# A perceiver block on one core: other steps for the interleaved stages of a batch, and a program of its own for the last batch's tail

## What is computed

```python
def _layernorm(x, eps=1e-05): ...
def cross(x, ctx):                      # x (4, 256, 256), ctx (4, 4096, 256), 16 heads of 16
    Q = x @ Wq.T + bq; K = ctx @ Wk.T + bk; V = ctx @ Wv.T + bv
    return softmax(Q K^T / sqrt(16)) V @ Wh.T + bh
def linear(x):                          # causal, random features
    q, k, v = split(x @ Wqkv + bqkv)
    def features(t):                    # R = 2, M = 32: 64 features for a head
        tn = t / norm(t)
        return exp(clip(tn @ omega[r] * sqrt(2 s[r]) - s[r], -20, 20)) / sqrt(M) * sqrt(weight[r])
    qf, kf = features(q), features(k)
    # out[t] = sum over t' <= t of (qf[t] . kf[t']) v[t'], over the same sum without v
    return out @ Wout + bout
def ffn(x):                             # integer weights x 1/127, hidden 768
    return (silu(x @ wg.T) * (x @ wu.T)) @ wd.T
x = x + cross(_layernorm(x), ctx)
x = x + linear(_layernorm(x))
x = x + ffn(_layernorm(x))
```

## Time and profile before

| | us |
|---|---|
| median of 3 runs | 904.28 (903.49 to 911.03) |
| the profiled execution | 905.16 |
| its span | 903.4 |
| PE busy | 842.8 (93%) |
| ACT busy | 533.5 (59%) |
| DVE busy | 425.4 (47%) |
| POOL busy | 48.4 (5%) |
| score products of batch 1 to 4 begin at | 29.85, 193.64, 402.42, 610.77 |
| the last value product ends at | 811.82 |

### The profile page before, as it was taken

How to read it: one execution, slowest core, us unless ns; L and a number is a source line. 1 busy time by engine, 2 the same in 40 slices (tenths; PEclk the granted TensorE clock), 3 DMA queues, 4 the chain that set the end, 5 groups by cost and what they waited for, 6 DMA issues and landing times.

```text
span 903.4 us, 20695 instructions
## 1 busy us (share of the span) xinstructions
PE 842.8 (93%) x8881; PEld 581.3 (64%) x8881; DVE 425.4 (47%) x751; ACT 533.5 (59%) x579; POOL 48.4 (5%) x76
## 2 busy tenths in 40 slices
PE   6899999999899999999899999999989999888876
PEld 6666666666566666676566666676656667657655
DVE  7433245545544446534644446434744444203663
ACT  2378787776467675656566665757556666760111
POOL 1034000000000000000000000000000000000000
PEclk9799999999999999999999999999999999999999
DMA  7487664656133334336333442446333331201000
GB/s 242 150 260 236 229 199 153 210 190 187 57 141 141 118 141 163 130 109 184 130 118 141 141 141 94 142 140 178 127 140 141 109 142 56 71 25 24 1 1 15
DMA packets 58736, 120.08 MB, mean 133 GB/s; under 512 B 21520, under 2 KB 29712, under 8 KB 55120
## 3 DMA queue, kind: packets, MB, share of 16 engines
q1 hardware_dynamic: 56848, 114.31, 37.2%
q0 software_dynamic: 1792, 4.40, 1.9%
HBM read 78.84 MB, written 37.75 MB: 129 GB/s over the span
## 4 chain that ended last, share of the span: by engine, by line
PE 77%; DVE 9%; issue 5%; DMA 4%; ACT 3%; DVEq 1%; POOL 1%; SPq 0%; POOLq 0%; ACTq 0%
PE ps_o L777 24%; PE ps_s L789 16%; PE ps_pa L576 10%; PE ps_pa L621 10%; ACT probs L1066 2%; PE ps_pa L747 2%; DMA oscr<-y 2%; PE ps_pa L722 2%; PE ps_pa L713 1%; DMA y<-oscr 1%; PE ps_pa L699 1%; PE ps_pa L651 1%; PE ps_pa L734 1%; PE ps_pa L643 1%; DVE kparts L1105 1%
## 5 line engine op out<-in xcount | busy, mean ns | idle before, releaser
L1066 ACT ACTIVATE probs<-ps_s 128x1024 f32<-128x1024 f32 x512 | 496.7, 1023 | 262.8 <-PE ps_s L789 254.4
L777 PE MATMUL ps_o<-probs,values 128*17 128x256 f32 x4096 | 257.6, 386 | 0.3 <-ACT probs L1066 0.3
L789 PEld LDWEIGHTS ps_s<-qstack,kstack 64*128 64x128 f32 x2048 | 139.1, 185 | 102.4 <-ACT probs L1066 53.2
L789 PE MATMUL ps_s<-qstack,kstack 64*128 64x256 f32 x2048 | 193.5, 307 | 7.0 <-ACT probs L1066 7.0
L777 PEld LDWEIGHTS ps_o<-probs,values 128*17 128x17 f32 x4096 | 104.4, 98 | 100.3 <-issue 12.8
L1103 DVE TENSOR_SCALAR kparts<-ps_pa,b_heads 128x512 fp32r<-128x512 f32 x64 | 48.0, 750 | 122.1 <-PE ps_pa L576 122.1
L1120 DVE TENSOR_TENSOR values<-ps_pa,bv_pair 128x512 f32<-128x512 f32 x64 | 44.1, 690 | 84.7 <-PE ps_pa L621 84.3
L621 PE MATMUL ps_pa<-wv_hi,ctx_hi 128*128 128x256 f32 x256 | 79.5, 310 | 2.6 <-DVE wv_lo L1091 2.2
L621 PE MATMUL ps_pa<-wv_lo,ctx_hi 128*128 128x256 f32 x256 | 73.2, 286 | 0.0
L621 PE MATMUL ps_pa<-wv_hi,ctx_lo 128*128 128x256 f32 x256 | 73.1, 286 | 0.0
L576 PE MATMUL ps_pa<-ctx_hi,wk_hi 128*128 128x512 f32 x128 | 56.5, 441 | 0.0
(11 more groups left out here) (252 smaller groups left out, 792.2 us busy)
## 6 DMA issues: line engine op xcount, KB each, us to landing
kstack<-kscr SPq DMA_DIRECT2D x96, 512.0 KB, 5.3
kscr<-kparts SPq DMA_DIRECT2D x64, 512.0 KB, 2.7
ctx_raw<-ctxT SPq DMA_DIRECT2D x32, 512.0 KB, 6.6
qstack<-qscr SPq DMA_DIRECT2D x12, 256.0 KB, 3.4
qscr<-qparts SPq DMA_DIRECT2D x4, 512.0 KB, 4.4
xh<-x SPq DMA_DIRECT2D x4, 256.0 KB, 5.6
kstack<-kstack SPq DMA_DIRECT2D x2, 512.0 KB, 6.0
qstack<-ksample SPq DMA_DIRECT2D x4, 256.0 KB, 3.6
```

What stands on the lines that cost most here:

```text
L777: last = mm(ps_o[32 * j:32 * j + DH + 1, g * S:(g + 1) * S], values[par][:, i, head_of_step(g, j), :], prob[:, j * S:(j + 1) * S], start=b ...
L789: last = mm(ps_s[s % 2][:, j * S:(j + 1) * S], kstack[par][rows, u, i * P:(i + 1) * P], queries[rows, u, :], start=True, stop=True)
L1066: nc.scalar.activation(probs[n % AHEAD][:, :], ps_s[n % 2][:, :], ACT.Exp, scale=float(DH) ** -0.5).then_inc(fast["exp_done"], 1)
```

## The change

It has three parts. In `AT` and `HEAD_AT` the stages get other steps: `qkT0`, `qkT1` from 26 and 28 to 28 and 30, the wide stages from 32 to 80 to 38 to 84, and what follows two to four steps later; `ln0T` from 92 to 94; `q` from 99 to 100; `down` from 122 to 124. Second, the last batch's tail no longer calls `stage()`: each engine has a program of its own, written out, in which work on 256 rows is done in two halves of 128 rows (t = 0, 1) with waits of their own, DVE and ACT each evicting one half; ACT squares for the norms, copies the last 128x128 block of each masked pair and the sums of `pv`; POOL weights the features; two gates are computed ahead of each `down` part; the writes, the reads and the stores go by half. Third, its warm-ups are 83 calls of `warm`'s product where they were 115, at other places.

```diff
-      "norm0": 26, "qkT0": 26, "norm1": 27, "qkT1": 28,
-      "feat0": 32, "feat1": 38, "A0": 42, "A1": 46, "feat2": 48, "pv0": 50, "A2": 54, "A3": 58, "pv1": 60, "feat3": 62,
-      "A4": 64, "A5": 70, "pv2": 72, "A6": 74, "A7": 78, "pv3": 80, "o2T0": 84, "o2T1": 86, "y2T": 88, "wout": 90,
-      "ln2T": 94, "gu0": 96, "gate0": 98, "gu1": 100, "gate1": 101, "gu2": 102, "gate2": 103, "gu3": 104, "gate3": 105,
-      "gu4": 106, "gate4": 107, "gu5": 110, "gate5": 111, "down": 122}
+      "norm0": 26, "norm1": 27, "qkT0": 28, "qkT1": 30,
+      "feat0": 38, "feat1": 42, "A0": 46, "A1": 48, "pv0": 52, "feat2": 54, "A2": 58, "A3": 62, "feat3": 64, "pv1": 66,
+      "A4": 70, "A5": 74, "pv2": 76, "A6": 78, "A7": 80, "pv3": 84, "o2T0": 86, "o2T1": 88, "y2T": 90, "wout": 92,
+      "ln2T": 96, "gu0": 99, "gate0": 101, "gu1": 102, "gate1": 103, "gu2": 104, "gate2": 105, "gu3": 106, "gate3": 107,
+      "gu4": 110, "gate4": 111, "gu5": 120, "gate5": 121, "down": 124}
 TAIL = list(AT)
-HEAD_AT = {"ln0": 86, "ln0T": 92, "q": 99, "kbd0": 106, "max0": 108, "kbd1": 110, "max1": 112, "max2": 115,
+HEAD_AT = {"ln0": 86, "ln0T": 94, "q": 100, "kbd0": 106, "max0": 108, "kbd1": 110, "max1": 112, "max2": 115,
            "max3": 116, "maxT": 118}
-WARM = {"yT": 30, "ln1T": 14, "qkT0": 22, "A0": 14, "y2T": 3, "ln2T": 12, "gu0": 3, "down": 5}
-WARM_JUDGED = 12
...
-            write_output(fast, tail_of(B - 1))
-            regroup_output(fast, B - 1)
-            store(fast, tail_of(B - 1), B - 1)
-
-            sp.wait_ge(fast["stored"], B * 16)
+            for t in range(ST):
+                sp.wait_ge(*vector_of(f"y{t}"))
+                sp.dma_start(oscr[:, t * P:(t + 1) * P, :].rearrange("h s d -> s h d"),
+                             y[:, t, :].rearrange("p (h d) -> p h d", h=H)).then_inc(fast["o_written"], 16)
+            sp.wait_ge(fast["o_written"], B * 32)
+            for t, landed in enumerate((fast["o_in"], o_in_last)):
+                sp.dma_start(y[:, t, :], oscr[t * HALF:(t + 1) * HALF, :, :].rearrange("a (u s) d -> (a u) (s d)", u=S // DH)
+                             ).then_inc(landed, 16)
...
+            warm(ps_p, 12)
             pe.wait_ge(judged, 1)
             nc.tensor.transpose(ps_a[0:1, 0:P], den_ok[:, 0:1], ident[:, :]).then_inc(judged, 1)
-            products(fast, TAIL[NORMALISED:], tail_of(B - 1), True)
+            warm(ps_p, 26)
+            pe.wait_ge(fast["o_in"], B * 16)
+            turn_rows(halves[2], 0, y).then_inc(last_product, 1)
+            pe.wait_ge(o_in_last, 16)
+            turn_rows(halves[3], 1, y).then_inc(last_product, 1)
+            for t in range(ST):
+                pe.wait_ge(*(scalar_of("yT1") if t else vector_of("yT0")))
+                rows_by(halves[4 + t], t, wh_sb, D).then_inc(last_product, 1)
+            warm(ps_p, 7)
...
+            warm(ps_o, 14)
+            for t in range(ST):
+                pe.wait_ge(*vector_of(f"norm{t}"))
+                for i in range(4):
+                    last = nc.tensor.transpose(halves[2 + t][:, i * P:(i + 1) * P], qk[:, t, i * P:(i + 1) * P], ident[:, :])
+                last.then_inc(last_product, 1)
...
+            warm(ps_o, 10)
+            pe.wait_ge(*vector_of("v"))
+            for g in range(G):
+                pe.wait_ge(*pool_of(f"feat{g}"))
+                last_pairs(2 * g)
+                if g:
+                    pe.wait_ge(*scalar_of(f"pv{g - 1}"))
+                last_pairs(2 * g + 1)
+                if g + 2 < G:
+                    pe.wait_ge(*vector_of(f"feat{g}"))
+                    last_features(g + 2)
+                if g == G - 1:
+                    for t in range(ST):
+                        for k in range(G - 1):
+                            nc.tensor.transpose(halves[t][:, k * P:(k + 1) * P], o_sb[:, k, t * P:(t + 1) * P], ident[:, :])
+                last_values(g)
...
+            for k in range(HB):
+                last_gates(k)
+                if k >= 2:
+                    last_down(k - 2)
+            for k in (HB - 2, HB - 1):
+                last_down(k)
...
+            def last_corner(n):
+                act.wait_ge(*vector_of(f"A{n}"))
+                bank = last_wide(f"A{n}")
+                nc.scalar.activation(amat[:, n % 2 * 2:n % 2 * 2 + 2, P:S],
+                                     bank[:, :].rearrange("p (e k) -> p e k", e=2)[:, :, P:S], ACT.Copy
+                                     ).then_inc(last_scalar, 1)
...
+            nc.scalar.activation(o_sb[:, G // 2:G, :], ps_o[:, 512:1024].rearrange("p (g s) -> p g s", s=S), ACT.Copy
+                                 ).then_inc(last_scalar, 1)
+            last_columns("yT1", "yT1", halves[3])
+            last_columns("ln1T1", "ln1T1", halves[3])
+            for t in range(ST):
+                act.wait_ge(*vector_of(f"qk{t}"))
+                nc.scalar.activation(feat[:, 0, t, :, :].rearrange("p c s -> p (c s)"), qk[:, t, :], ACT.Square
+                                     ).then_inc(last_scalar, 1)
...
+            def last_masks(n):
+                dve.wait_ge(*product_of(f"A{n}"))
+                blocks = last_wide(f"A{n}")[:, :].rearrange("p (e b k) -> p e b k", e=2, k=P)
+                into = amat[:, n % 2 * 2:n % 2 * 2 + 2, :].rearrange("p e (b k) -> p e b k", k=P)
+                v.tensor_tensor(into[:, :, 0:3:2, :], blocks[:, :, 0:3:2, :],
+                                causal[:, 0:P].unsqueeze(1).unsqueeze(1).to_broadcast([P, 2, 2, P]), ALU.mult
+                                ).then_inc(last_vector, 1)
```

More of the change, by code:

```diff
@@ L895, in _, with turn_rows, rows_by @@
             values_up_to(B * BS)
-            products(fast, TAIL[:NORMALISED], tail_of(B - 1), True)
-            warm(ps_p, WARM_JUDGED)
+            def turn_rows(bank, t, rows):
+                for i in range(CI):
+                    last = nc.tensor.transpose(bank[:, i * P:(i + 1) * P], rows[:, t, i * P:(i + 1) * P], ident[:, :])
+                return last
+            def rows_by(bank, t, w, n, col=0):
+                for k in range(CI):
+                    last = mm(bank[:, 0:n], xT[:, k, t * P:(t + 1) * P], w[:, k, col:col + n], start=k == 0, stop=k == CI - 1)
+                return last
@@ new lines, in last_pairs @@
+            def last_pairs(n):
+                f, bank = n // 2, last_wide(f"A{n}")
+                for first, at in ((0, 0), (P, S)):
+                    for e in range(2):
+                        rows64 = slice(e * ROWS, (e + 1) * ROWS)
+                        last = mm(bank[:, e * 512 + at:e * 512 + at + S - first], kfeat[rows64, f % 2, n % 2, first:first + P],
+                                  feat[rows64, f % 2, n % 2, 0, first:S], start=True, stop=True, skip_group_check=True)
+                last.then_inc(last_product, 1)
@@ new lines, in _ @@
+            warm(ps_p, 7)
+            for t in range(ST):
+                pe.wait_ge(*vector_of(f"xn1_{t}"))
+                turn_rows(halves[2 + t], t, xn).then_inc(last_product, 1)
+            for t in range(ST):
+                pe.wait_ge(*(scalar_of("ln1T1") if t else vector_of("ln1T0")))
+                rows_by(halves[t], t, wqkv_sb, 2 * D).then_inc(last_product, 1)
+            for t in range(ST):
+                last = rows_by(ps_p[:, t * D:(t + 1) * D], t, wqkv_sb, D, 2 * D)
+            last.then_inc(last_product, 1)
@@ new lines, in _ @@
+            warm(ps_p, 7)
+            for t in range(ST):
+                pe.wait_ge(*vector_of(f"xn2_{t}"))
+                for i in range(CI):
+                    last = nc.tensor.transpose(halves[2][:, i * S + t * P:i * S + (t + 1) * P], xn[:, t, i * P:(i + 1) * P],
+                                               ident[:, :])
+            last.then_inc(last_product, 1)
+            warm(ps_p, 4)
+            pe.wait_ge(*vector_of("ln2T"))
+            for k in range(HB):
+                last_gates(k)
+                if k >= 2:
+                    last_down(k - 2)
@@ L1426, in _ @@
+            for t in range(ST):
+                dve.wait_ge(*product_of(f"down{t}"))
+                v.scalar_tensor_tensor(y[:, t, :], (ps_p, ps_a)[t][:, 0:D], QUANT ** 3 / 2, xs[:, t, :], ALU.mult, ALU.add
+                                       ).then_inc(last_vector, 1)
             dve.wait_ge(judged, 3)
```

255 lines of the change are left out of this document (242 added, 13 removed).

## The result

The changed kernel takes 878.71 us, the median of 4 runs (875.48 to 880.65), against 906.18 for the kernel before beside it; the ratio is 0.9688, 95% interval 0.9631 to 0.9745. Forecast was 876.6, range 869 to 886. The profiled execution took 875.48, the fastest of the four; its span is 873.8, before it was 903.4.

What follows compares the result with a forecast made beforehand. TensorE's work, busy 93% of the span, sets the batches' pace; the last tail is one engine-to-engine chain. Span 903.4 - 15.0 + 2.8 - 0.5 - 15.0 = 875.7 us, so 876.6 us measured, range 869 to 886.

Steps and rivals of the forecast that it cites:

- The stall at the transposes and the wide stages: Batches two to four: PE's idle before `qkT0` and `feat0` and the half clock go, 5.0 us a batch, 15.0 in three.
- a cover that fails: Wide stages: 1.6 us of scores and values should hide evictions; if they do not, 0.6 us lost a batch.
- The term for the clock, 1.45: Behind the idle at `qkT0`: 32 value matmuls at half clock take 3.37 us instead of 1.92; 1.45 gained a batch.
- `ln0T`: Second and third batch: PE waits longer there for `wout`'s layernorm, idle 2.35 us for 1.40, +0.95.
- the +0.2 for that quad: `q` now ahead of `gu1` in one quad: 0.5 us for its four evictions, less the 0.3 it waited itself.
- `down` in the fourth batch: `down` moves behind the last quad's scores, so the last value products find their exponentials ready: -0.5 us.
- The rival of a moved stall: Idle at `ln0T` followed by half clock, 1.45 us twice: 879.5; with later waits at wide stages 885. Chance 14%.
- half clock in the gates: One of the signs named beforehand that would show the forecast wrong; no size given.
- The tail: From the last value product to the end: nine stretches shorten by 15.5 us, less 0.5 for a store, -15.0.
- the reason for the pairs: Tail, first pair product to first denominator: shorter VectorE masks, corners and pv copies on ScalarE; 15.7 us for 18.56, gain 2.9.
- The tail's clock: Last tail: two stretches at half clock already counted, no further fall expected; one stretch costs at most 1.7 us.
- The rival of a cold tail: Last tail: fewer warm-ups, three half-clock stretches instead of two, half the pair gain lost; 5 to 8 us, 882 to 885. Chance 12%.

Runs made afterwards that it cites:

- experiment 3: The changed kernel with `norm0`, `qkT0`, `norm1` and `qkT1` back at their old steps (26, 26, 27, 28): 891.08 us, ratio 0.9805 to the kernel before.
- experiment 5: The changed kernel with `ln0T` waiting for its own layernorm and the addition reading `wout`'s bank, not `wout`'s whole layernorm: 873.93 us, ratio 0.9632.
- experiment 7: The changed kernel with 14 warm-ups instead of 26 ahead of `yT` in the last tail: 875.13 us, ratio 0.9646.
- experiment 9: The changed kernel with VectorE masking all three blocks of a pair and no corner copies on ScalarE: 879.66 us, ratio 0.9670.
- experiment 10: The changed kernel with the tail's later features behind the values again and one gate, not two, ahead of each down part: 883.23 us, ratio 0.9739.
- experiment 2: The changed kernel with the old step tables, so that only the last tail is new: 888.38 us, ratio 0.9801 to the kernel before.
- experiment 4: The changed kernel with `ln0T` at step 96 instead of 94: 877.91 us, ratio 0.9693.
- experiment 11: The changed kernel run again without any edit: 876.82 us, ratio 0.9678 to the kernel before.
- experiment 6: The changed kernel with `ln0T` at step 91, behind `y2T` and ahead of `wout`: 879.45 us, ratio 0.9687.
- experiment 12: The changed kernel with `ln0T` on the earlier signals and 14 warm-ups ahead of `yT`, together: 871.48 us, ratio 0.9617.
- experiment 8: The changed kernel without any of the 83 warm-up calls in the last tail: 885.90 us, ratio 0.9778.

## Why the prediction was right, and where not

- **The stall at the transposes and the wide stages** (5.0 a batch): right. Up to step 55 batch 3 is 6.2 shorter, 1.1 of which is a pair stage (`A2`) that now runs later, so 5.1; experiment 3 brings 14.5 in three batches back with the transposes alone. The wide stages gained more than was counted: 0.59 of idle in the quad of step 64 went too, in each batch, which the forecast named as the price of a cover that fails and not as a gain. Their move was not undone by itself. The term for the clock, 1.45, should have been 1.8: 4.3 measured for the two quads, less 2.46 of idle.
- **`ln0T`** (+0.95): idle 2.35 forecast, 2.33 and 2.68 measured, so +1.3 in both batches. The reason given, that it needs `wout`'s layernorm, failed: it needs the signal, not the data (experiment 5). What cannot be moved is VectorE's load. `y2T` (+0.3) did not wait at all; `gu1` behind `q` waits 0.66, where `q` and `gu2` waited 0.32 and 0.29, so the +0.2 for that quad is about right.
- **`down` in the fourth batch** (-0.5): did not come. PE waits 1.30 in each of the quads of steps 116 and 120 before and after, and 0.29 and 0.23 in the last.
- **The rival of a moved stall** came in part: behind 2.68 the clock fell in 6 of the 8 executions profiled with `ln0T` at 94 and its old wait (both of the changed kernel among them), behind 2.33 in one of 8. It was priced at 1.45 and took 2.9 where two pieces of 3.4 us came together (3.3 more in the quads than in batch 2, 0.35 of it the longer idle). The forecast's centre had none of this, and the median came out 2.1 above it. One of its signs of being wrong, half clock in the gates, came too, though not in the tail: behind a wait of 1.74 at `gu3` of batch 4, in 9 of the 12 profiles with the new tables (not in that of the result). And its remark that the trace ends each stretch of half clock after 3.4 us overlooks one of 6.8 at the start (22.7 us).
- **The tail** (15.0): 14.7. The 15.0 were 15.5 by stretches less 0.5 for a wait of `oT0` on a store, and that wait did not come (PE waits 0.81 there, for VectorE's copy), so the stretches gave 0.8 less than their sum. Seven of nine are right to 0.2. That the warm-ups and not the read set `yT` is shown by experiment 7; the read was there at 9.0, the early end of the stated 9.0 to 10.6. **Wrong was the reason for the pairs:** the step put the gain of 2.9 on shorter masks with the corner on ScalarE, and experiment 9 gives nothing of it back. 1.8 of it is `feat3` ahead of the values, so that its clip falls into VectorE's gap; experiment 10 takes 1.6 for each stage so placed. The other 1.1 may be the copies of the sums on ScalarE; that was not tried. The end, forecast 0.3 shorter, is 0.5 longer as the table counts it; from the last half's addition at 869.02 it is 4.8, as long as before. Its store starts as the second of two on SP; what that costs was not tried.
- **The tail's clock** ("no further fall"): none in the profiled execution, but one or two pieces of 3.4 us between `feat0` and the first pair in experiments 2, 4, 5, 9, 10 and 11, 0.7 to 1.5 us, and in 3, 6, 7 and 12 none. The rival of a cold tail (5 to 8 us) did not come; without any warm-ups (experiment 8) it does, with 6.9 us.
- **ScalarE's copies** out of PSUM take 383 ns for 128x256 and 597 for 128x512, VectorE's 425 and some 690, as the forecast took them. The Trainium skill (ScalarE: Activation LUTs, Rules for kernel authors) sends `relu`, `max`, `min`, `add` and `mul` to VectorE; it does not name copies, and for these evictions the rows do not bear such a choice out.

That the sum of the batches came out to 0.1 is luck. Where the clock does not fall at `ln0T` or later, and without the waits for the transfer at `yT`, batches 2 to 4 are 4.8, 4.5 and 6.4 shorter (read for the last two from experiments 8 and 4), 15.6 in all for 12.7. In the profiled execution half clock took 2.9 back at `ln0T` and 1.6 in batch 4, and shorter waits at `yT` gave 1.7, which have no cause in the change: these waits are between 0 and 1.8 in the profiles, also of the same program.
